# A two-block transformer kernel: the second mixture of experts for the two chosen experts alone, behind the loop

## The reference

```python
logits = jnp.einsum('bsd,ed->bse', x, router_w)
probs = jax.nn.softmax(logits, axis=-1)
topk_vals, topk_idx = jax.lax.top_k(probs, K)          # K = 2 of E = 8
for eid in range(e):
    w = jnp.sum(jnp.where(idx == eid, vals, 0), axis=-1)
    h = jax.nn.gelu(x_flat @ w1[eid].T, approximate=False)
    y = h @ w2[eid].T
    out = out + w[:, None] * y
```

## Time and profile before

| | |
|---|---|
| median of 3 runs | 1448.29 us (1448.22 to 1450.28) |
| the profiled execution: its own time | 1447.02 us |
| its span, first to last instruction | 1445.2 us |
| mean granted TensorE clock | 0.988 of full |
| PE busy | 1375.4 us, 95% |
| PE weight loads busy | 1203.8 us, 83% |
| DVE busy | 928.1 us, 64% |
| ACT busy | 903.1 us, 62% |
| POOL busy | 498.9 us, 35% |
| moved by DMA | 13.77 MB, nearly all in the first 36 us |

### The profile page before, as it was taken

The page is one execution under the profiler, slowest core; times in us unless marked ns, Lnnn a source line. Parts: engine busy times, 40 slices in busy tenths (PEclk is TensorE's granted clock), DMA queues, the critical chain, the costliest instruction groups (busy, mean ns, idle before and its releaser), DMA issues.

```text
span 1445.2 us, 33202 instructions
## 1 busy us (share of the span) xinstructions
PE 1375.4 (95%) x11328; PEld 1203.8 (83%) x11328; DVE 928.1 (64%) x2535; ACT 903.1 (62%) x2492; POOL 498.9 (35%) x409
## 2 busy tenths in 40 slices
PE   5797999999999999999999999999999999999768
PEld 4585989888898988889898898988889898888767
DVE  4456567575666757576675756667575675756683
ACT  4665775757566575766757576575757757575423
POOL 2307053160714417062350706225070531607100
PEclk9999999999999999999999999999999999999988
DMA  7000000000000000000000000000000000000000
GB/s 259 1 5 1 5 2 8 0 2 5 0 7 0 7 0 0 7 0 7 0 7 0 0 7 0 7 0 7 0 0 7 0 7 0 2 3 1 5 1 8
DMA packets 14088, 13.77 MB, mean 10 GB/s; under 512 B 1625, under 2 KB 12770, under 8 KB 13794
## 3 DMA queue, kind: packets, MB, share of 16 engines
q1 hardware_dynamic: 14050, 13.27, 2.9%
HBM read 11.17 MB, written 2.10 MB: 9 GB/s over the span
## 4 chain that ended last, share of the span: by engine, by line
PE 64%; issue 13%; DVE 8%; ACT 4%; DVEq 4%; POOL 3%; POOLq 2%; DMA 0%; SPq 0%; ACTq 0%
PE bank_F L1204 14%; PE bank_S L1074 6%; DVEq L343 4%; PE bank_T L1115 4%; PE bank_A L1128 4%; PE bank_T L1060 3%; ACT probs L566 3%; PE bank_A L1139 3%; PE bank_T L1061 3%; PE bank_T L1062 3%; PE bank_A L1060 3%; PE bank_A L1061 3%; PE bank_A L1062 3%; PE bank_F L1060 2%; PE bank_F L1062 2%
## 5 line engine op out<-in xcount | busy, mean ns | idle before, releaser
L1204 PE MATMUL bank_F<-down,hid 128*128 128x128 f32 x2944 | 356.0, 276 | 7.1 <-DVE x L783 6.4
L1204 PEld LDWEIGHTS bank_F<-down,hid 128*128 128x128 f32 x2944 | 341.5, 192 | 17.2 <-DVE x L783 9.9
L566 ACT ACTIVATE probs<-bank_S,neg_max 128x256 f32<-128x256 f32 x512 | 235.9, 475 | 143.6 <-DVE neg_max L704 143.6
L704 DVE TENSOR_REDUCE neg_max<-bank_S 128x2 f32<-128x512 f32 x256 | 164.7, 685 | 96.3 <-PE bank_S L1074 96.2
L783 DVE SCALAR_TENSOR_TENSOR x<-bank_F,gates,x 128x128 f32<-128x128 f32 x496 | 150.1, 344 | 42.5 <-PE bank_F L1204 32.7
L485 POOL TENSOR_TENSOR hid<-hid,qkv 128x1024 f32<-128x1024 f32 x60 | 169.1, 2828 | 22.7 <-ACT hid L582 22.7
L455 POOL TENSOR_TENSOR mean_sq<-sum_sq,one_over_d 128x2 f32<-128x2 f32 x16 | 3.1, 195 | 453.4 <-ACT h_row L540 453.4
L545 ACT ACTIVATE probsT<-bank_T 128x512 f32<-128x512 f32 x256 | 139.4, 605 | 28.0 <-PE bank_T L1115 28.0
L473 POOL TENSOR_TENSOR hid<-qkv 128x1024 f32<-128x1024 f32 x45 | 121.1, 2692 | 69.2 <-ACT qkv L545 69.2
L1139 PE MATMUL bank_A<-probsT,values 128*64 128x256 f32 x1024 | 140.4, 395 | 1.1 <-ACT probsT L545 1.0
L1115 PE MATMUL bank_T<-ident,probs 128*128 128x128 f32 x1024 | 138.3, 278 | 0.1
(11 more groups left out here) (191 smaller groups left out, 3233.2 us busy)
## 6 DMA issues: line engine op xcount, KB each, us to landing
x_row<-in_x SPq DMA_DIRECT2D x16, 128.0 KB, 2.1
down<-in_w SPq DMA_DIRECT2D x1, 2048.0 KB, 15.4
out<-x SPq DMA_DIRECT2D x16, 128.0 KB, 1.8
hid<-in_w SPq DMA_DIRECT2D x1, 1536.0 KB, 7.9
hid<-in_rw SPq DMA_DIRECT2D x1, 1024.0 KB, 7.4
hid<-in_wv SPq DMA_DIRECT2D x1, 512.0 KB, 3.9
hid<-in_wq SPq DMA_DIRECT2D x1, 512.0 KB, 4.8
hid<-in_wk SPq DMA_DIRECT2D x1, 512.0 KB, 5.5
```

What stands on the lines that cost most here:

```text
L566: ins = sc.activation(probs[:, h // 2 % 2, h % 2, t, :], unit.bank(f"S{h}")[:, t * S:(t + 1) * S], ACT.Exp, bias=neg_max[:, h, t:t + 1], a ...
L704: ve.tensor_reduce(neg_max[:, h, :], v.bank(f"S{h}")[:, :].rearrange("p (t k) -> p t k", t=NT), AX.X, ALU.max, negate=True).then_inc(max_r ...
L1204: ins = te.matmul(bank[:, (j * NT + t) * P:(j * NT + t + 1) * P], hid[:, e, k, tokens(t)], down[:, e, k, :], start=k == 0, stop=k == m - 1)
```

## The change

The second mixture leaves the loop and is done for the chosen experts alone:

- In the loop, for row `it - 2`: its norm (step 1 of the eight), `X3T` as one copy (step 3), the router (step 4), and new, `RK` and `place_row` (steps 5 and 6): products of a triangular matrix with the mask of chosen experts give each token its rank within its expert. The gate follows behind `OUT`. `U1_*`, `D1e*`, the 16 `mix` operations and the last norm leave it. The row stays in SBUF (`x3`, 16 rows).
- Rows 0 to 9 and 10 to 14 are two groups. When a group is ranked, `map_blocks` (some 16 small VectorE operations, in iterations 12 and 16) gives each expert whole blocks of 128 places, 47 blocks at most for the first group and 27 for the second, and each token two places. GpSimd scatters each row by four indirect DMAs (two halves, two choices) to a buffer in HBM that was filled with zeros: rows 0 to 3 at the end of iteration 12, 4 to 6 in 13, 7 to 9 in 14, the second group in the tail.
- Behind the loop a stream of pairs of blocks: SyncE loads two blocks of tokens (128 KB, in runs of 512 bytes) and, by an expert number that it reads from the map, 512 KB of weights for each block (`w12`, 4 KB for each partition), in a ring of four pairs; TensorE transposes, multiplies up (4 float32 matmuls of 128 columns for a block) and down (4); ScalarE copies, takes gelus, copies out; SyncE stores the result over the block. The list goes by pairs: `XT` of the pair after next, `UB` twice, `DB` of the pair before.
- Row 15 is done by all eight experts at the end (16 blocks, each expert's weights loaded once), and added up as before.
- GpSimd gathers each row's two results (four indirect DMAs a row), VectorE weights and adds them (`combine`), the last norm follows, and all 16 rows are stored then.
- The work between: `tail` in iteration 16 does the first mixture and the small attention of row 15, row 14's router and rank, the second map; some of it stands among the pairs (`BESIDE`).
- In the part behind `OUT`: `QK0`, `V0` and `V1` go ahead of `X1T`, `V3` behind `S1`; VectorE's order there is new; the small attention has buffers of its own, and GpSimd no longer adds the halves of the value products, which VectorE now sums in full.
- The hardware loop is gone: all iterations are written out. The loads of the first mixture's down weights and later ones are issued behind the load of row 1; those of the second mixture are gone.

```diff
-FILL_C = {(2, 1): ["D1e0"], (4, 1): ["D1e1"], (5, 1): ["D1e2"], (6, 1): ["D1e3"], (7, 0): ["D1e4"], (7, 1): ["D1e5"]}
+FILL_C = {(2, 1): ["X3T"], (4, 0): ["R1"], (5, 1): ["RK"]}
+FILL_MAP = {(2, 1): ["CN"]}
+BESIDE = {0: ["CN"], 1: ["X2T"], 2: ["LQ0", "LQ1"], 12: ["AOT"], 13: ["PROJ"], 15: ["X3E"], 16: ["R1E"]}
...
+        put("A", "D0p0", "D0p1", "X3T", "D0p2", "WT0", "R1", "D0p3", "D0base", "RK")
+        put("B", "XT0", "XT1")
+        for p, (_, blocks) in enumerate(PAIRS):
+            put("B", f"XT{p + 2}", on=p + 2 < SPARSE)
+            put("B", *[f"UB{p}_{j}" for j in range(len(blocks))])
+            put("B", f"DB{p - 1}", on=p > 0)
+            put("A", *BESIDE.get(p, []))
+        put("B", f"DB{len(PAIRS) - 1}")
...
+    put("A", f"O{HP - 1}", "OUT")
+    put("A", "QK0", on=nxt)
+    put("G", "V0", "V1", on=nxt)
+    put("A", "X1T")
+    put("G", "V2", on=nxt)
+    put("G", "U0_0", "U0_1")
+    put("A", "R0")
+    put("G", "U0_2", "U0_3", "U0_4", "U0_5")
+    put("A", "QK1", on=nxt)
     put("G", "AOT", on=b)
-    put("G", "U0_4", on=a)
+    put("G", "U0_6", "U0_7")
     put("G", "PROJ", on=b)
+    put("G", "U0_8")
     put("S0", "S0", on=nxt)
     put("S1", "S1", on=nxt)
+    put("G", "V3", on=nxt)
...
+            def load_pair(v, p):
+                g, blocks = PAIRS[p]
+                if p < SPARSE:
+                    if blocks[0] == 0:
+                        sp.wait_ge(map_ready, g + 1)
+                        sp.wait_ge(scattered[g], 16 * 2 * NT * len(GROUPS[g]))
+                    if p >= RING:
+                        sp.wait_ge(*v.fill(f"XT{p - RING}"))
+                    sp.dma_start(xb[:, p % RING, 0:len(blocks), :], xs[g][blocks[0]:blocks[-1] + 1, :, :].rearrange("b s d -> s b d")).then_inc(xb_in[p % RING], 16)
+                if p >= RING:
+                    sp.wait_ge(*v.fill(f"DB{p - RING}"))
+                for j in range(n_weights(p)):
+                    slot = p % RING * 2 + j
+                    if p < SPARSE:
+                        expert = sp.value_load(block_map[0:1, g, blocks[j]:blocks[j] + 1], min_val=0, max_val=E - 1)
+                        src = w12_in[bass.ds(expert, 1), :, :]
+                    else:
+                        src = w12_in[p - SPARSE:p - SPARSE + 1, :, :]
+                    sp.dma_start(w_slots[slot], src.rearrange("a h c -> h (a c)")).then_inc(w_loaded[slot], 16)
...
+            def gather(row):
+                i = group_of(row)
+                if row == GROUPS[i][0]:
+                    for p in range(last_pair(i) - RING + 1, last_pair(i) + 1):
+                        pool.wait_ge(y_out[p % RING], 16 * ring_uses(p))
+                for t in range(NT):
+                    for c in range(2):
+                        g.indirect_dma_start(yg[:, row % YG_RING, t, c, :], None, xs[i].rearrange("b s d -> (b s) d"),
+                                             bass.IndirectOffsetOnAxis(ap=slots_of[:, row, t, c:c + 1], axis=0)).then_inc(gathered[row % YG_RING], 16)
...
# VectorE, the part behind OUT
+                residual(v, "OUT", x1[:], x_plus[:])
+                ln_stats(0, x1[:])
+                if v.next:
+                    first_pair(v, 0)
                 if v.b:
                     head_softmax_sum(v, 0)
+                ln_apply(0, x1[:], v.at(0, 1, 1))
+                transposed_out(v, "X1T", None, x1T)
                 if v.b:
                     head_softmax_sum(v, 1)
+                    head_out(v, 0)
+                first_route(v)
                 if v.b:
+                    head_out(v, 1)
+                if v.next:
+                    first_pair(v, 1)
                 if v.b:
                     transposed_out(v, "AOT", aoT[:])
                 if v.c:
+                    second_gate(v.it - 2)
                 if v.b:
+                    second_in(v)
                 if v.next:
                     head_max(v, 0)
                     head_max(v, 1)
...
# VectorE, the end of the tail
+                for e in range(E):
+                    dense_mix(v, e)
+                    if e < len(GROUPS[1]):
+                        combine(GROUPS[1][e])
+                        if e >= 2:
+                            out_norm(GROUPS[1][e - 2])
+                for r in GROUPS[1][-2:]:
+                    out_norm(r)
+                out_stats(row)
+                out_norm(row)
```

More of the change, by code:

```diff
@@ L333, in run @@
                 before(Before(banks))
[L334 to L338 removed]
+            for it in range(ROWS + 1):
                 body(Iteration(it, 0, banks))
@@ L664, in body @@
                         head_exp(v, 0)
+                    if v.c and s == 5:
+                        router_exp(v, 1)
                 if v.b:
@@ L679, in body @@
                     v_out(v, 3)
-                if v.b and v.next:
-                    for u in range(2 * E):
-                        gelu1(v, u)
             def before(v):
@@ new lines, in unit @@
+                if name[:2] == "UB":
+                    p, j = (int(n) for n in name[2:].split("_"))
+                    slot = p % RING * 2 + (j if p < SPARSE else 0)
+                    pe.wait_ge(w_loaded[slot], 16 * weight_uses(p, slot % 2))
+                    pe.wait_ge(*v.drain(f"XT{p}" if p < SPARSE else "X3E"))
+                    xT = xbT[:, p % RING, tokens(j)] if p < SPARSE else x3T[:, tokens(j)]
+                    for m in range(M1):
+                        ins = te.matmul(bank[:, m * P:(m + 1) * P], w_slots[slot][:, m * P:(m + 1) * P], xT, start=True, stop=True)
+                    return ins
```

742 lines of the change are left out of this document (465 added, 277 removed).

## The result

The changed kernel took 1579.21 us in the median (1572.17 to 1581.15, four runs) where the kernel before took 1448.78 beside it: ratio 1.089, 95% interval 1.0854 to 1.0925. The forecast was 1427, its range 1368 to 1482: wrong in sign and outside the range. The profiled execution took 1577.88, 1576.1 of it span.

The account below looks back on a forecast made before the run. TensorE's sequence of turns was taken as the bound. From a span of 1445.2: -5.3 -1.9 -139.6 (loop) +6 (map, gates) +119.2 (tail) = 1423.6, so 1426.7 us in the median, 1.5% faster; range 1368 to 1482.

Parts of the forecast that it names:

- A: Up to the first output projection: ScalarE's 5.6 us wait for row 1 goes, -5.3 us, to 59.5.
- B: From iteration 0's output projection to iteration 1's: 67.6 us instead of 69.5.
- C, first stretch: Fourteen iterations, output projection to first exponential: VectorE's list sets 25.4 us, where it was 35.9.
- C, second stretch: Fourteen iterations, first exponential to next output projection: iteration 1's 46.8 us plus 3.3, so 50.1; route counted at 2.0.
- The written-out loop costs nothing: Whole loop: writing out all iterations adds no time, as iterations 0, 1 and 15 already were.
- Scatters hidden: End of iteration 12: 16 scatter issues lie in GpSimd's idle stretch; at up to 1.7 us each nobody waits.
- D, the stream's pace: Stream behind the loop: 4.0 us a pair, set by TensorE; loads 3.6, SyncE 2.9.
- D, the start: Behind the last output projection: the stream's first block starts at 35 us, with 3 more for small units.
- D, gathers: Tail: 1.2 us a gather; first group gathered by 187 us behind the last output projection, second by 221.
- The loads set the pace: Rival, stream: loads slow each pair to 6.2 us, adding 81 us, to 1508; chance 0.12.
- The clock: Rival, loop: TensorE's clock drops at the hole ahead of AOT, units 3.5 us later, +56, 1483; chance 0.11.
- Gathers at 2 us an issue: Rival, tail: slower gather issues on GpSimd add 38 us, to 1465; chance 0.08.

Follow-up runs that it names:

- e9: The changed kernel with a pair's tokens loaded two pairs ahead on SyncE's queue, on a chip without the stall: 1516.25 us, ratio 1.0469.
- e10: The changed kernel with tokens two pairs ahead and epsilon's addition moved to VectorE, so no GpSimd drain between rows' gathers, without the stall: 1485.12 us, ratio 1.0254.
- b1: The kernel before with only the later weights' loads issued behind row 1's load: 1446.84 us, ratio 0.9989.
- e11: e10 with the second route one step later (step 5 instead of 4), behind GpSimd's products: 1464.75 us, ratio 1.0125.
- e12: e10 with GpSimd's products of queries and keys cut to one head of eight from iteration 3 on: 1464.83 us, ratio 1.0126.
- e3: The changed kernel with GpSimd's products of queries and keys cut to one head of eight from iteration 3 on: 1599.66 us.
- c2: The kernel before with its loop written out, nothing else: 1451.47 us, ratio 1.0023.
- e5: The changed kernel with tokens two pairs ahead and all 60 scatters behind the loop: 1575.57 us.
- c1: The changed kernel, unaltered, as a control; it ran without the stall: 1575.64 us, ratio 1.0874.
- e4: The changed kernel with the second route a step earlier (X3T's copy in step 2, route in step 3): 1686.02 us.
- e1: The changed kernel with a pair's tokens loaded two pairs ahead on SyncE's queue, nothing else moved: 1565.21 us.
- c4: The changed kernel, unaltered, as a control on a chip where it had the stall: 1619.63 us.

## Why the prediction was wrong, point by point

Three terms failed: the second `route` at 2.0 us (some 42 us of the loop), the stream's pace of 4.0 us, costed without the order of SyncE's queue (79 us), and the gathers, costed without GpSimd's drains (31 us by e9 and e10).

- **The bound of the kernel before**: right. TensorE's share of the chain fell to 20%, iterations from 85.5 to 78.4.
- **A** (59.5) and **B** (67.6): 58.5 and 67.5, right in size. b1 shows that the reason given for A is not enough alone: in the kernel before the same move gives 1.3 us, because GpSimd's weight split takes the wait's place; in the changed kernel the split stands at 20.1 to 25.2 and the norm at 40.3.
- **C, first stretch** (25.4): 25.1 to 25.7 in iterations 2 to 13. The terms as listed come to 23.7 and 25.1, not 23.9 and 25.4, which changes nothing here. Adding up VectorE's list from single rows works where it stands nearly gapless.
- **C, second stretch** (50.1, bounds 47.5 to 51.8): 53.2, outside the bounds. The term that failed is "`route` 2.0 in step 4". It took 3.5, with `head_product` ahead of it at 2.41 (1.36 in iteration 1, from which the 46.8 comes), since each two-operand operation waits for GpSimd's instruction of the moment. The prediction read durations from places where GpSimd did not stand in their way. Over iterations 2 to 15 the excess, 3.1 us in most, is some 42 of the loop's 45 us. e11 and e12 show the cause by two ways, for the second stretch: it falls to 50.2 to 51.4. But the first one grows meanwhile, and e11 gives back 23.8 us of the 42; why the first one grows is open (in e3 the clock goes with it, in e11 26.9 and 27.0 stand at 0.94 as well).
- **"The written-out loop costs nothing"**: 3.4 us by c2, in the kernel before. **Map and split of gates** (6): right. Iterations 12 and 13 took 3.7 and 5.7 more than their neighbours, 9.4, but 3.7 and 2.5 in e5, whose iteration 13 has no scatters.
- **"Scatters hidden"**: nearly right where there is no stall. Where there is, the loop takes 34 us more (1270.4 against 1236.2); where there is none, they cost 4 to 5, by e5 against c1. No rival of the prediction had it.
- **D, the stream's pace** (4.0): its parts were right, as e9 and e10 went the 37 steps in 143.0 and 143.8 us at TensorE's pace, with 348 GB/s. What failed is the sentence that TensorE sets the pace: the SyncE queue was costed by the length of its issues (2.9), and not by what stands in it behind which wait. Had the order of `blocks_through` been played through, tokens one pair ahead against a landing of several us would have shown it. This is 79 of the tail's 107 us (232.9 against 154).
- **D, the start** (first block 35, first `DB` 38): 39.8 and 43.9, +6, with clock 0.84. What set it was not tested.
- **D, gathers** (1.2 each, second group gathered 27 behind the stored results at 195): 1.26 each, but the drain that `settled` puts into `inverse_out` was not priced. The prediction counted GpSimd's issues and passed over its drains. With the drain away the sum for D holds within 13 us, in part by luck: e10 has 246.5 where 233.5 was forecast, but 43.9, 143.8 and 58.8 for the three parts forecast at 38, 154 and 41.5.
- **The rivals.** "The loads set the pace" gave 6.2 a pair and 1508, and the measured pace was 6.3, but by another mechanism: not transfers at their limit, since DMA was busy 64%. The Trainium skill's fit (DMA: Bandwidth & Descriptors, Anatomy of one DMA), measured for DMAs that GpSimd issues and worked out one at a time to an estimate of 6.4 us a pair, comes equally near without being the cause; e10 moves the same 512 KB loads, issued by SyncE, at 143.8 / 37 = 3.9 a pair, so their size did no harm here. "The clock": it did fall in every iteration from 2 on, behind the hole ahead of `X1T` and again in the second stretch, as the rows of iteration 7 below this list show (PE's timeline, then columns as above). Yet the first exponential came at 25.1 to 25.7, so that the 3.5 us of this rival did not come. That the 6.8 us at half speed cost the second stretch nothing is not shown: e3's second stretches took 50.2 us at 0.97 and 51.3 at 0.93. "Gathers at 2 us an issue": false as told, yet 31 us were lost there to the drain. The change ended on the rivals' side because two of them were right in effect at once; each had been given its chance as if alone.

```profile
604.56 0.41 PE L1364 MATMUL bank_A<-ident,x 128*128 128x128 f32 x2 [2.36 <-DVE x L952]
```

```profile
604.90:608.30 3.40, 3.40 (x14) 2.74 (x13) 3.00 (x6) 1.16 (x3) 0.32 (x1) 0.50 0.16 43
659.50:666.30 6.80, 5.07 (x29) 3.31 (x28) 5.39 (x10) 4.01 (x14) 0.93 (x2) 0.50 0.01 2
```

Put together: 1427 + 45 (loop) + 6 (start) + 79 (pairs) + 22 (rest of the tail) = 1579. After all three repairs the change still ends 1.25% above the kernel before: 418 us of TensorE's work in the loop bought 118 us of it (1330.9 - 1213.0), and the tail grew from 114 to 247.6. The head stretch waits for VectorE's list, and the tail is a chain of stream, gathers and combination.

## What to carry to other kernels

Play a queue through in its own order, at least over two rounds: a ring of four buffers looks ahead as far as the first wait that stands before the load, here one pair. Read a duration where its engine's neighbours do what they will do beside it: operations of VectorE with two operands in SBUF, and here `TENSOR_SCALAR` from SBUF to SBUF too, cost what GpSimd's current instruction has left. Before such an operation is moved, look at what GpSimd does at the new place: e4 moved it into the products, e11 out of them. And price every drain of GpSimd behind an indirect DMA as the landing of that DMA.

## What the runs showed of the hardware

- A GpSimd drain behind four gathers lasted 1.6 to 4.6 us in the kernel after, until the last had landed; without it sixty gathers came 1.41 us apart in the mean (e10), 1.26 within a row.
- The same kernel took 1575.6 and 1579.7 us on two chips and 1619.6 on a third, the kernel before 1448.0, 1447.6 and 1448.1 beside it. The difference lies in TensorE, which on one kind ran one matmul every 1.4 us (e1, 1033 to 1039) once scatters had followed one another for 8 us (c4). e1 to e4 ran on a fourth chip, with that stall. What makes a chip, or the placing of a program on it, one or the other stays open.
- A float32 subtraction of 128 x 16 took 0.18 us alone, 1.61 and 2.38 beside a product of GpSimd's; a `TENSOR_SCALAR` of 128 x 128 took 0.28 alone and 6.01 beside a GpSimd operation of 6.69.
- Two loads of 512 KB, 128 KB of tokens and 128 KB of results a pair went at 348 GB/s with TensorE at 98% and a granted clock of 1.00 (e10).
